# Combine phase: the query projection in three products of rounded high and low parts

## The reference

```python
x = x + 0.5 * ffn(layernorm(x))
x = x + attention(layernorm(x))
x = x + 0.5 * ffn(layernorm(x))
```

```python
out = _mha(x, o, o, c_Wq, c_bq, c_Wk, c_bk, c_Wv, c_bv, c_Wo, c_bo)
# qh = (q @ Wq + bq), softmax over 16 slots for each of 16 heads, attn @ vh, @ Wo + bo
```

## Time and profile before

| | us |
|---|---|
| median of 3 runs (2523.58 to 2525.71) | 2524.52 |
| profiled execution, its own time | 2526.13 |
| profiled execution, its span | 2523.7 |
| TensorE busy in the span | 2343.7 |
| VectorE busy | 1866.2 |
| GpSimd busy | 1497.8 |
| ScalarE busy | 1460.5 |

### The profile page before, as it was taken

How to read it: one execution, slowest core, us unless ns; L and a number is a source line. 1 busy time by engine, 2 the same in 40 slices (tenths; PEclk the granted TensorE clock), 3 DMA queues, 4 the chain that set the end, 5 groups by cost and what they waited for, 6 DMA issues and landing times. The chain is left out here.

```text
span 2523.7 us, 54984 instructions
## 1 busy us (share of the span) xinstructions
PE 2343.7 (93%) x17368; PEld 1813.7 (72%) x17368; DVE 1866.2 (74%) x3259; ACT 1460.5 (58%) x3733; POOL 1497.8 (59%) x1268
## 2 busy tenths in 40 slices
PE   7986799799999999999999999999999969977998
PEld 5753477577787788788787887887888846743676
DVE  6751277578888898888788898888888857731576
ACT  2321244377787777777677777777777723311343
POOL 1100255398788888887787887888888901100442
PEclk9998899899999999999999999999999989997999
DMA  7359654366666566566566566566566655559443
GB/s 253 121 205 400 233 195 158 86 170 173 166 183 168 163 179 174 163 178 172 150 184 169 162 179 171 160 181 172 167 174 177 165 147 196 205 235 382 136 151 104
DMA packets 336760, 460.89 MB, mean 183 GB/s; under 512 B 63201, under 2 KB 273761, under 8 KB 332385
## 3 DMA queue, kind: packets, MB, share of 16 engines
q1 hardware_dynamic: 336480, 457.47, 59.9%
HBM read 279.09 MB, written 111.15 MB: 155 GB/s over the span
## 5 line engine op out<-in xcount | busy, mean ns | idle before, releaser
L1381 POOL TENSOR_TENSOR att_z_sb<-att_z_sb,att_cos 128x512 f32<-128x512 f32 x255 | 357.9, 1404 | 213.1 <-DMA att_zs<-att_z_sb 213.0
L1384 POOL TENSOR_TENSOR att_z_sb<-att_z_sb,att_zs 128x512 f32<-128x512 f32 x255 | 362.1, 1420 | 20.0
L1382 POOL TENSOR_TENSOR att_zs<-att_zs,att_sin 128x512 f32<-128x512 f32 x255 | 358.9, 1407 | 0.0
L1588 ACT ACTIVATE att_last<-att_ps_w,att_nmax 128x512 f32<-128x512 f32 x256 | 173.7, 683 | 220.0 <-DVE att_nmax L1478 190.9
L1588 ACT ACTIVATE att_prob<-att_ps_x,att_nmax 128x384 f32<-128x384 f32 (+1 forms) x512 | 237.8, 485 | 0.0
L1762 PE MATMUL att_ps_p<-att_probT,att_v_sb 128*64 128x384 f32 (+2 forms) x1536 | 195.4, 390 | 6.6 <-DVE att_lastT L1496 6.6
L1008 POOL TENSOR_TENSOR com_b_kblk<-sh_blkmask,sh_kT 128x128 f32<-128x128 f32 x64 | 32.8, 533 | 267.2 <-POOLq L477 220.2
L1389 POOL TENSOR_TENSOR att_kT_lo<-att_z_sb,att_kT_hi 128x512 fp32r<-128x512 f32 x128 | 163.7, 1279 | 38.7 <-ACT att_kT_hi L1574 38.7
L1603 ACT COPY att_probT<-att_ps_p 128x512 f32<-128x512 f32 x256 | 151.3, 591 | 45.7 <-PE att_ps_p L1748 41.8
L1762 PEld LDWEIGHTS att_ps_p<-att_probT,att_v_sb 128*64 128x64 f32 x1536 | 99.9, 137 | 102.9 <-issue 84.1
L180 POOL TENSOR_SCALAR dis_b_veps<-dis_b_mv 128x4 f32<-128x4 f32 x32 | 13.4, 418 | 266.6 <-DVE dis_b_mv L174 266.6
(11 more groups left out here) (231 smaller groups left out, 7291.8 us busy)
## 6 DMA issues: line engine op xcount, KB each, us to landing
att_zs<-att_z_sb SPq DMA_DIRECT2D x512, 128.0 KB, 2.4
last_tile_blocks<-att_last SPq DMA_DIRECT2D x128, 512.0 KB, 3.5
att_got<-last_tile_blocks SPq DMA_DIRECT2D x512, 128.0 KB, 2.9
ffn_w<-in_e_W SPq DMA_DIRECT2D x56, 1024.0 KB, 13.6
att_R<-inverse_sums SPq DMA_DIRECT2D x256, 128.0 KB, 4.3
ffn_wg<-in_e_Wg SPq DMA_DIRECT2D x24, 1024.0 KB, 13.9
x_normalised_transposed<-dis_b_xnT SPq DMA_DIRECT2D x32, 512.0 KB, 2.7
dis_b_x<-in_x SPq DMA_DIRECT2D x16, 512.0 KB, 4.4
```

Source lines behind the costliest of these rows:

```text
L1381: nc.gpsimd.tensor_tensor(z[:, m, i, :], z[:, m, i, :], cos[:], ALU.mult)
L1382: nc.gpsimd.tensor_tensor(zs[:, m, i, :], zs[:, m, i, :], sin[:], ALU.mult).then_inc(sin_s[i].sem, 1)
L1384: nc.gpsimd.tensor_tensor(z[:, m, i, :], z[:, m, i, :], zs[:, m, i, :], ALU.add).then_inc(sum_s[i].sem, 1)
L1588: nc.scalar.activation(dst, src, ACT.Exp, bias=nmax[:, p % 2, qt, hh:hh + 1], accum_out=sums[:, p % 2, hh, qt:qt + 1]).then_inc(exp_s.sem, 1)
```

## The change

In both combine phases the query projection no longer multiplies fp32 by fp32. The weight is split once into a rounded high part and the remainder (`weight`, `com_w_hi` and `com_w_lo` in the program's names), by DVE at the start of the phase. The tokens of every batch are split in the same way (`tokens`, `com_x_hi` and `com_x_lo`): ACT makes the high part (`token_high`), POOL the low part (`token_low`), two batches ahead of the scores. The projection is then three products: high by high, weight low by token high, and weight high by token low. Each is one fp32r matmul for each of the two chunks of 128 features, so six matmuls stand where two fp32 matmuls stood. The table of the halved output bias is now made in place, in `bo`.

```diff
-                        hold(g, sp, q_mm.sem, q_mm.at(v.u, DC))
+                        hold(g, sp, lo_s.sem, lo_s.at(v.u, DC))
                         load_t(unit(k, i + 2))
...
             dve.wait_ge(tab_in, 32)
-            nc.vector.tensor_scalar(boh[:], bo[:], 0.5, None, ALU.mult).then_inc(half_s, 1)
+            nc.vector.tensor_copy(weight[0][:], g.cwq[:]).then_inc(half_s, 1)
+            dve.wait_ge(half_s, WEIGHT_HI)
+            nc.vector.tensor_tensor(weight[1][:], g.cwq[:], weight[0][:].bitcast(F32), ALU.subtract).then_inc(half_s, 1)
+            nc.vector.tensor_scalar(bo[:], bo[:], 0.5, None, ALU.mult).then_inc(half_s, 1)
...
+            def token_low(v):
+                for ch in range(DC):
+                    pool.wait_ge(hi_s.sem, hi_s.at(v.u, ch + 1))
+                    nc.gpsimd.tensor_tensor(tokens[1][:, v.par, ch, :], xnT[v.par][:, ch, :], tokens[0][:, v.par, ch, :].bitcast(F32),
+                                            ALU.subtract).then_inc(lo_s.sem, 1)
...
                     if not last or i + 1 < NB:
                         residual(unit(k, i + 1))
+                    if not last or i + 2 < NB:
+                        token_low(unit(k, i + 2))
                     for h in range(2):
                         if ahead and split_step(first, last, i, h, 1) is not None:
                             ahead.low(pool, nc.gpsimd, split_step(first, last, i, h, 1), 1)
...
+            token_low(unit(0, 0))
             keys(unit(0, 0))
             values(unit(0, 0))
-            pool.wait_ge(half_s, 1)
+            pool.wait_ge(half_s, BIAS)
+            token_low(unit(0, 1))
             residual(unit(0, 0))
...
             def queries(v, m):
                 if m == 0:
-                    pe.wait_ge(xt_in[v.par], (v.k * (NB // 2) + v.i // 2 + 1) * 16)
+                    pe.wait_ge(hi_s.sem, hi_s.at(v.u, DC))
                 pe.wait_ge(q_s.sem, q_s.at(v.u, m - 1))
-                for ch in range(DC):
-                    last = nc.tensor.matmul(ps_q[m][:], g.cwq[:, ch, m * P:(m + 1) * P], xnT[v.par][:, ch, :],
-                                            start=(ch == 0), stop=(ch == DC - 1))
+                for a, b in ((0, 0), (1, 0), (0, 1)):
+                    if m == 0 and b == 1:
+                        pe.wait_ge(lo_s.sem, lo_s.at(v.u, DC))
+                    for ch in range(DC):
+                        last = nc.tensor.matmul(ps_q[m][:], weight[a][:, ch, m * P:(m + 1) * P], tokens[b][:, v.par, ch, :],
+                                                start=(a + b + ch == 0), stop=(b == 1 and ch == DC - 1))
...
+            pe.wait_ge(half_s, WEIGHT_LO)
             for m in range(DC):
                 queries(unit(0, 0), m)
...
             act.wait_ge(tab_in, 32)
+
+            def token_high(v, ch):
+                if ch == 0:
+                    act.wait_ge(xt_in[v.par], (v.k * (NB // 2) + v.i // 2 + 1) * 16)
+                    if not isinstance(v.u, int) or v.u >= 2:
+                        act.wait_ge(q_mm.sem, q_mm.at(v.u, DC - 2 * DC))
+                nc.scalar.copy(tokens[0][:, v.par, ch, :], xnT[v.par][:, ch, :]).then_inc(hi_s.sem, 1)
...
                         if following:
                             evacuate(unit(k, i + 1), h)
+                        if not last or i + 2 < NB:
+                            token_high(unit(k, i + 2), h)
...
+            for i in range(2):
+                for ch in range(DC):
+                    token_high(unit(0, i), ch)
             for m in range(DC):
                 evacuate(unit(0, 0), m)
             values(unit(0, 0))
```

More of the change, by code:

```diff
@@ L876, in combine_phase @@
     pt_mm, pt_s, o_mm, o_s = c("pt_mm", 2, 2), c("pt", 2, 1), c("o_mm", 2, 1), c("o", 2, 2)
+    hi_s, lo_s = c("x_hi", DC), c("x_lo", DC)
+    WEIGHT_HI, WEIGHT_LO, BIAS = 1, 2, 3
     unit = lambda k, i: Unit(NB, k, i)
@@ L880, in combine_phase @@
         pb = lambda nm, sh: s.enter_context(nc.psum_tensor(name(nm), sh, F32))
-        bq, bo, boh = sb("t_bq", [P, DC, P]), sb("t_bo", [P, W, D]), sb("t_boh", [P, W, D])
+        bq, bo = sb("t_bq", [P, DC, P]), sb("t_bo", [P, W, D])
         xin = [x0] + [sb(f"b_x{i}", [P, TT, D]) for i in range(1, RX)]
         xnT = [xt0] + [sb(f"b_xnT{i}", [P, DC, S]) for i in range(1, RT)]
+        rounded = lambda nm, sh: [s.enter_context(nc.sbuf_tensor(name(f"{nm}_{x}"), sh, F32R)) for x in ("hi", "lo")]
+        weight, tokens = rounded("w", [P, DC, D]), rounded("x", [P, 2, DC, S])
         qT, xo = sb("b_qT", [P, 2, DC, S]), sb("b_xo", [P, 2, W, D])
@@ L1023, in residual @@
                     t = xin[v.i][:, 2 * h:2 * h + 2, :]
-                    last = nc.gpsimd.tensor_tensor(t, t, boh[:], ALU.add)
+                    last = nc.gpsimd.tensor_tensor(t, t, bo[:], ALU.add)
                 last.then_inc(xb_s.sem, 1)
```

## The result

The changed kernel takes 2542.23 us (median of 5, 2538.14 to 2545.48), the kernel before 2525.71 us on the same chip (median of 5, 2523.58 to 2527.91). The ratio is 1.0065, 95% interval 1.005 to 1.008: slower by 16.5 us. The forecast's sum was 7 us, and the time lies just inside the upper end of its range, 2543.

What follows compares the result with a forecast made beforehand. The prediction took PE to bound the kernel (busy 145.00 of 145.00 us in combine 2). Combine 2 at +0.4 and combine 1 at +6.8 gave +7 us, so 2531.5, stated as 2531 us; range 2518 to 2543.

Steps and rivals of the forecast that it cites:

- Term 1: PE's queries in both combine phases: six products take 1.38 us against 1.72, a batch 9.73, 0.68 us less.
- Term 2: DVE's softmax product waits for POOL's residual in alternate batches; 0.27 us a batch remains saved, -4.0 us over combine 2.
- The walk: Batch timing from a fold's end: product asked for at 4.32 waits to 5.4, batch 10.55 us; next batch 9.73, alternating.
- A collision in every batch: Rival: the product meets a whole residual each batch, 10.55 or 10.9 us a batch; total 2543; chance 0.15.
- Term 3: Start of each combine phase: casts wait for both tables, low parts follow, first fold later; +4.4 us a phase.
- Term 4: Combine 1: eight batches -2.1 us, seven save nothing, late deviation +4 and low clock +0.5; with the start +6.8.

Runs made afterwards that it cites:

- all four edits: Changed kernel with residual before values, tables' wait moved later, deviation early, and each phase's first residual held behind the first product: 2506.83 us, ratio 0.9928.
- three edits: Changed kernel with residual before values, tables' wait behind the casts and weight split, and deviation at the start of GpSimd's third batch: 2509.1 us, ratio 0.994.
- no low part: Changed kernel without GpSimd's subtraction for the tokens; the third product reads the tokens' high part again: 2516.08 us, ratio 0.9963.

## Why the prediction was right, and where it was short

**Term 1 held.** 1.82 us from the transposes to the mix in place of 2.16, and 9.75 us for a batch wherever nothing collides; 9.73 was forecast.

**Term 2 held for one batch and failed for the next.** The walk gave, behind the end of a fold, the low part's end at 1.0, the product's request at 4.32, the residual's end at 5.4, the batch at 10.55. Behind the fold that ends at 2429.76 the rows have 1.0, 4.31, 5.4 and, for the batch, 10.49. The step that failed is "Because PE slipped by 0.8 and POOL did not, the next batch finds the boundary between the two residuals". POOL did slip: its second low part waits for ACT's cast, the cast stands behind the evacuation of PE's queries, and so POOL's place is tied to PE's. The walk used this dependence to place POOL in the first batch and forgot it in the second. The second batch of combine 2 escapes (9.75 us) and the third takes 10.31; from then on the collision comes in every batch, at some 10.49 us, and the 14 batches gain nothing (+0.3 us; -4.0 forecast for 15). This was the rival "A collision in every batch". Its counter-argument, that PE's slip moves the two apart, is the same mistake.

**Term 3 held**: +4.7 and +4.8 us, +4.4 forecast. Moving the wait for the tables took 3.2 and 3.3 us back, so most of this term was the tables and not the longer chain of casts and low parts.

**Term 4 held for the deviation.** Its batch costs +4.4 us, +4.5 forecast, and the edit that moves the deviation returns 3.4 of it alone. The other 13 batches gained 4.1 us, 2 more than forecast, and that total hides two misses. The eight batches of the loop were to gain 2.1 and lost 0.2 (they collide as in combine 2). The five in the first and last bodies, where "nothing saved" was the forecast, gained 4.3: the last two take 9.76 and 9.75 us in place of 10.82. In these two no product holds PE up.

**What no term held** is the first batch of each phase, 4.7 us each, 9.4 together. The prediction said "the first batches of a phase meet fewer" collisions and rounded down for it. They meet the costliest one. Its other mistake here is the sentence "a DVE operation with both inputs in SBUF waits for a whole POOL instruction, up to 1.25 us": that bound was read from single collisions, and the first product waited for three.

The sum was +7 us, the two phases show +19.1: 9.4 from the first batches and 4.3 from the other batches of combine 2 are missing, and combine 1's other batches give 2 back. The direction rested on the starts and the deviation, which were read rightly. That the time lies in the range is in part luck: its upper end, 2543, was the price of the rival with a collision in every batch, which had +12 us for combine 1 (the folds show +9.4) and nothing for a first batch, and the measured time is below it by 0.8 us only. The 19.1 us of the two phases alone, on the 2524.5 of the kernel before, would be 2543.6.

## What to carry to other kernels

When one engine's work is tied to another's by a semaphore, a slip of the first moves the second with it, and a collision does not resolve by itself: walk two batches, with every wait of both, before counting on an alternation. GpSimd work that fits easily into a batch by its busy time can still cost all that the change saves; give it the place in the order where VectorE has no operation with two inputs in SBUF due, or hold it behind that operation with a semaphore (here, by the medians, the first took 10.6 us of the 16.5 away, the second 8.2). And a new consumer at the start of a phase should wait for its own data, not for the phase's tables.

## What the runs showed of the hardware

**A waiting VectorE operation can be passed over.** In the collisions read in the steady batches the product is served at the end of the POOL instruction that runs when it asks (wait of 0.97 us in the rows above), and the next POOL instruction waits. The first product of a phase, asked for 0.3 us into the first of three POOL instructions, was served only behind the third, at POOL's first idle time: 3.95 and 4.01 us in the changed kernel, 3.96 to 4.22 in four others. (With the residual ahead of the values, in combine 1, it was asked for as the residual's first half ended, and served behind four more instructions.) But not always: with the deviation early the same code took 4.20 us in combine 1 and 1.56 in combine 2. What decides it stays open. A satisfied wait between the instructions changes nothing. Nor does the position of the request, as far as the timelines resolve it: the product of 1.56 us was asked for 0.25 us into the residual, those of 4.01 and 3.95 us 0.26 and 0.30 into it. By SBUF — State Buffer in the Trainium skill (Who interferes with whom) whoever issues first gets the shared pair for one whole instruction; the steady batches agree with that, and the page says nothing of a request that is passed over.

**An operation with one input can wait as well.** The scaling of the bias table, SBUF to SBUF in fp32, took 1.50 us beside GpSimd's low parts (row at 2356.05) and 0.43 before. The same section of the Trainium skill names `tensor_scalar` with copy and cast among the operations that "can all enter" modes with two ports and can then contend, if their operands meet its conditions; the 1.50 us agree. The addition with one input in PSUM shows no such wait: 0.68 us in the earlier trace rows.

**The clock behind an idle time.** At the same place of the first batch PE stayed at 2.4 GHz behind an idle time of 1.72 us (with the first residual held back, queries of 0.62 us for two products) and of 1.76 (all four edits, combine 2), and fell to 1.2 GHz behind 1.94 (three edits) and 1.88 (all four edits, combine 1). The batch then took 9.77 and 9.76 us, or 11.52 and 11.46. So 0.1 to 0.2 us of waiting more was followed by 1.7 us of batch. At other places the length of the idle time alone doesn't tell the two apart. Behind the normalisation PE stayed at full clock after 2.25 us (no low part) and fell after 1.88 (the kernel before). At the end of combine 1 every kernel idles 1.1 and then 0.7 us; the mix behind it took 1.99 us in three of the ten and 2.87 to 3.68 in the others. The rows of three edits, where the clock fell, and of no low part, where it stayed:

```profile
2344.30 0.82 PE L1104 MATMUL com_ps_pt<-sh_ident,com_b_prob 128*128 128x128 f32 x4 [1.94 <-DVE com_b_prob L979]
2344.77 1.20 PE L1083 MATMUL com_ps_q<-com_x_hi,com_w_hi 128*128 128x512 f32 x2
```

```profile
450.00 0.66 PE L1099 MATMUL com_ps_pt<-sh_ident,com_b_prob 128*128 128x128 f32 x4 [2.25 <-DVE com_b_prob L979]
450.41 0.71 PE L1078 MATMUL com_ps_q<-com_x_hi,com_w_hi 128*128 128x512 f32 x2
450.96 0.63 PE L1078 MATMUL com_ps_q<-com_x_hi,com_w_lo 128*128 128x512 f32 x2
```
